# Value products in halves, the causal triangle inside the row maximum, and a moved turn of the maxima

## What is computed

```
att = einsum('bqhd,bkhd->bhqk', q, k) / sqrt(hd)      # L1_ffn, twice (f1, f2): 32 heads of 4, all keys
scores = einsum('bqhd,bkhd->bhqk', q, k) / sqrt(hd)   # L1_attn, L2_attn (a1, a2): 16 heads of 8
scores = scores + triu(-inf, k=1)                     # causal, in a1 and a2 alone
out = softmax(scores) @ v
```

## Time and profile before

| | us |
|---|---|
| runs | 3000.34, 3005.62, 3008.44 (median 3005.62) |
| profiled execution | 2999.32 |
| its span | 2997.6 |
| PE, PEld, DVE, ACT, POOL busy | 90%, 35%, 76%, 61%, 18% of the span |
| L1357 row maxima | 1566.9 us busy, 1536 instructions |
| L1232 exponentials | 1382.6 us busy, 2816 instructions |
| L972 value products | 712.9 us busy, 5632 instructions (an f32 product is two) |

### The profile page before, as it was taken

The page is one execution under the profiler, slowest core; times in us unless marked ns, Lnnn a source line. Parts: engine busy times, 40 slices in busy tenths (PEclk is TensorE's granted clock), DMA queues, the critical chain, the costliest instruction groups (busy, mean ns, idle before and its releaser), DMA issues. The chain is left out here.

```text
span 2997.6 us, 44120 instructions
## 1 busy us (share of the span) xinstructions
PE 2711.8 (90%) x16188; PEld 1052.7 (35%) x16188; DVE 2293.0 (76%) x3000; ACT 1830.7 (61%) x3731; POOL 530.3 (18%) x847
## 2 busy tenths in 40 slices
PE   5989898899999999889978999999998889979778
PEld 2437443122222222633332222222226433336336
DVE  5456545999999997667758999999984767765993
ACT  2213323588888888546655888888885656655203
POOL 0000001110111000122312110101001323222771
PEclk9999999799999999989987999999999889989989
DMA  3210121300000000221114000000000221100000
GB/s 116 85 62 2 53 89 56 120 20 20 20 20 20 18 14 25 79 64 47 39 31 138 20 20 16 16 20 20 20 18 21 78 63 39 39 29 29 0 0 16
DMA packets 71968, 120.38 MB, mean 40 GB/s; under 512 B 16905, under 2 KB 44041, under 8 KB 68586
## 3 DMA queue, kind: packets, MB, share of 16 engines
q1 hardware_dynamic: 71754, 117.57, 12.1%
HBM read 94.19 MB, written 23.33 MB: 39 GB/s over the span
## 5 line engine op out<-in xcount | busy, mean ns | idle before, releaser
L1357 DVE TENSOR_REDUCE arena<-ps 128x1 f32<-128x1024 f32 (+7 forms) x1536 | 1566.9, 1063 | 216.9 <-PE ps L952 136.9
L1232 ACT ACTIVATE arena<-ps 128x512 f32<-128x512 f32 (+3 forms) x2816 | 1382.6, 573 | 373.9 <-PE ps L1036 372.9
L946 PE MATMUL ps<-arena 61*128 61x512 bf16 (+4 forms) x2816 | 943.2, 383 | 42.7 <-DVE arena L1357 14.8
L1036 PE MATMUL ps<-arena 64*128 64x512 bf16 (+4 forms) x2816 | 746.8, 372 | 63.6 <-ACT arena L1232 40.4
L972 PE MATMUL ps<-arena 128*32 128x512 f32 (+3 forms) x5632 | 712.9, 578 | 0.4 <-POOL arena L1316 0.3
L1036 PEld LDWEIGHTS ps<-arena 64*128 64x128 bf16 (+1 forms) x2816 | 206.9, 95 | 788.3 <-ACT arena L1232 549.0
L946 PEld LDWEIGHTS ps<-arena 61*128 61x128 bf16 (+1 forms) x2816 | 261.2, 96 | 346.5 <-DVE arena L1357 284.0
L347 PE MATMUL ps<-xnT,moe_up 128*128 128x512 f32 x448 | 216.5, 609 | 0.0
L1285 POOL TENSOR_TENSOR arena<-arena,ones 16x128 bf16<-16x128 f32 x96 | 42.7, 445 | 953.9 <-ACT arena L1217 901.5
L463 ACT ACTIVATE arena<-ps 128x512 f32<-128x512 f32 x112 | 66.5, 597 | 208.0 <-PE ps L347 208.0
L533 DVE TENSOR_TENSOR arena<-arena,ps 128x512 f32<-128x512 f32 x112 | 76.5, 686 | 148.6 <-ACT arena L463 120.7
(11 more groups left out here) (241 smaller groups left out, 2504.5 us busy)
## 6 DMA issues: line engine op xcount, KB each, us to landing
arena<-m_w SPq DMA_DIRECT2D x40, 256.0 KB, 3.0
arena<-f_q SPq DMA_DIRECT2D x60, 144.0 KB
arena<-f_k SPq DMA_DIRECT2D x180, 48.0 KB
arena<-in_w SPq DMA_DIRECT2D x4, 2048.0 KB
arena<-a_q SPq DMA_DIRECT2D x14, 576.0 KB
arena<-a_k SPq DMA_DIRECT2D x42, 192.0 KB
a_q<-arena SPq DMA_DIRECT2D x44, 96.0 KB, 2.0
a_k<-arena SPq DMA_DIRECT2D x44, 96.0 KB, 2.0
```

What stands on the lines that cost most here:

```text
L946: last = nc.tensor.matmul(at[:, k0 // CHUNK, 0:n], score_rows(Qop[par], j, slice(q0, q0 + P)), score_rows(Kop[par], j, slice(k0, k0 + n)), ...
L1036: nc.tensor.matmul(ps[:, ring_bank(item), off:CHUNK], shifted_rows(Kop[par], j, slice(kb * P, (kb + 1) * P)), shifted_rows(Qop[par], j, sl ...
L1232: nc.scalar.activation(pr[:, (at % 2) * 4 + j, off:CHUNK], ps[:, ring_bank(item), off:CHUNK], ACT.Exp).then_inc(s.ex, 1)
L1357: nc.vector.tensor_reduce(mq[:, half, j * 4 + qb:j * 4 + qb + 1], src, AXX, ALU.max).then_inc(s.sread, 1)
```

## The change

Full layers: `ST_ORDER` becomes 0, 1, 2, 3. The AV of a step is split in two products of 256 queries each; the first is issued behind the second ST and its piece, the second at the end. An AV of key block 0 stays whole, at the end, since it starts the accumulation. All waits of an AV move to its first half; only the second half counts up `s.av`.

Causal layers: L952 is gone. The row maximum becomes one VectorE instruction that reads the scores (PSUM) and a bf16 tile `causal_add` (SBUF: zeros and the triangle), writes the sum back over the scores and gives its maximum. `causal_add` is made once per causal layer by a memset of 448 words and a copy of 128 columns.

Both: the turn is issued behind the piece or task that follows its score tile, not ahead of it.

```diff
--- before.py
+++ after.py
@@ -665,6 +665,7 @@
             mT = c(P)
             mr = c(P)
             ms = c(2 * 3 * P, BF16).rearrange("p (n a t) -> p n a t", n=2, a=3)
+            causal_add = None if full else c(SEQ, BF16)
 
             rot = c((4 if rope else 0) * CHUNK).rearrange("p (m n t) -> p m n t", m=2, n=2) if rope else None
             rem_at = c.at
@@ -872,7 +873,7 @@
                 for u in range(UNITS):
                     unit(u, u // 3, u % 3, u + 2 < UNITS, u + 1 < UNITS)
 
-            ST_ORDER = [0, 2, 1, 3] if SIDES == 2 else [0, 1, 2, 3]
+            ST_ORDER = [0, 1, 2, 3]
             S_ORDER = [2, 0, 3, 1] if SIDES == 2 else [0, 1, 2, 3]
 
             def s_tasks(half):
@@ -946,11 +947,7 @@
                         last = nc.tensor.matmul(at[:, k0 // CHUNK, 0:n],
                                                 score_rows(Qop[par], j, slice(q0, q0 + P)),
                                                 score_rows(Kop[par], j, slice(k0, k0 + n)), start=True,
-                                                stop=full or k0 + n < width)
-                    if not full:
-                        off = (width - P) % CHUNK
-                        last = nc.tensor.matmul(at[:, (width - 1) // CHUNK, off:off + P], identb[:, :],
-                                                maskb[:, 0, :], start=False, stop=True)
+                                                stop=True)
                     if piece != 0:
                         last.then_inc(s.s, 1)
 
@@ -960,21 +957,27 @@
                     nc.tensor.transpose(ps[0:16, bank, 0:P], mq[:, hn % 2, :], ident[:, :])\
                         .then_inc(s.mtp, 1)
 
-                def attend(u, vpar, at):
+                def attend(u, vpar, at, half=None):
                     qc, kb, off = steps[at]
-                    pe.wait_ge(s.ex, u * 4 * NS + 4 * at + 4 + 3)
+                    if half == 0 and kb == 0:
+                        return
+                    cols = slice(off, CHUNK) if half is None or kb == 0 else \
+                        slice(half * (CHUNK // 2), (half + 1) * (CHUNK // 2))
+                    if half != 1 or kb == 0:
+                        pe.wait_ge(s.ex, u * 4 * NS + 4 * at + 4 + 3)
                     if at in diagonal:
                         pe.wait_ge(s.tri, u * len(diagonal) + diagonal.index(at) + 1)
                     if kb == 0:
                         pe.wait_ge(s.vx, u + 1)
                         pe.wait_ge(s.ocp, 2 * u + qc + 1)
                     for j in range(GROUP):
-                        last = nc.tensor.matmul(ps[32 * j:32 * j + 32, O_BANK, off:CHUNK],
+                        last = nc.tensor.matmul(ps[32 * j:32 * j + 32, O_BANK, cols],
                                                 vx[vpar][:, kb, j, :],
-                                                pr[:, (at % 2) * 4 + j, off:CHUNK],
+                                                pr[:, (at % 2) * 4 + j, cols],
                                                 start=kb == 0, stop=at in ends,
                                                 tile_position=(0, 32 * j), skip_group_check=True)
-                    last.then_inc(s.av, 1)
+                    if half != 0:
+                        last.then_inc(s.av, 1)
 
                 def out_project(ch, n):
                     if n == 0:
@@ -1030,6 +1033,12 @@
                             n_task, piece = task
                             scores(n_task, piece=piece)
 
+                        def values_behind(half):
+                            if at:
+                                attend(u, par, at - 1, half)
+                            elif u:
+                                attend(u - 1, (par + 2) % 3, NS - 1, half)
+
                         for i, j in enumerate(ST_ORDER):
                             item = ("st", u * 4 * NS + 4 * at + i)
                             ring_free(pe, item)
@@ -1039,17 +1048,16 @@
                                 shifted_rows(Qop[par], j, slice(qc * CHUNK + off, (qc + 1) * CHUNK)),
                                 start=True, stop=True).then_inc(s.st, 1)
                             turn = ("turn", 2 * u + 1 + qc)
+                            if (SIDES == 2 or i % 2) and todo:
+                                run(todo.pop(0))
                             if (kb, i) == TURN_AT[qc] and turn in ring_at:
                                 ring_free(pe, turn)
                                 turn_max(turn[1], ring_bank(turn))
-                            if (SIDES == 2 or i % 2) and todo:
-                                run(todo.pop(0))
+                            if full and i == 1:
+                                values_behind(0)
                         while todo:
                             run(todo.pop(0))
-                        if at:
-                            attend(u, par, at - 1)
-                        elif u:
-                            attend(u - 1, (par + 2) % 3, NS - 1)
+                        values_behind(1 if full else None)
                         if u == UNITS - 1 and at >= NS - 2 * TPC:
                             out_project((at - NS + 2 * TPC) // TPC, (at - NS + 2 * TPC) % TPC)
                     if not ahead1:
@@ -1354,8 +1362,12 @@
                         b = score_bank(half, k)
                         width = SEQ if full else half * CHUNK + (qb + 1) * P
                         src = ps[:, b:b + 2, :].rearrange("p b t -> p (b t)")[:, 0:width]
-                        nc.vector.tensor_reduce(mq[:, half, j * 4 + qb:j * 4 + qb + 1], src, AXX,
-                                                ALU.max).then_inc(s.sread, 1)
+                        top = mq[:, half, j * 4 + qb:j * 4 + qb + 1]
+                        if full:
+                            nc.vector.tensor_reduce(top, src, AXX, ALU.max).then_inc(s.sread, 1)
+                        else:
+                            nc.vector.tensor_tensor_reduce(src, src, causal_add[:, SEQ - width:], 1.0, -3.0e38,
+                                                           ALU.add, ALU.max, top).then_inc(s.sread, 1)
 
                 def rotate(ch, side):
                     tt = slice((ch % 2) * CHUNK, (ch % 2 + 1) * CHUNK)
@@ -1390,6 +1402,9 @@
 
                 norm_chunk(dve, s, t, x_rows, 0)
                 norm_chunk(dve, s, t, x_rows, 1)
+                if not full:
+                    nc.vector.memset(causal_add[:, 0:SEQ - P].bitcast(F32), 0.0)
+                    t.settle(dve, nc.vector.tensor_copy(causal_add[:, SEQ - P:], maskb[:, 0, :]))
                 if rope:
                     dve.wait_ge(s.tab, 16)
                 cutting(0)
```

## The result

The changed kernel takes 2902.3 us (median of four runs, 2901.0 to 2904.1) against 3003.6 us before (four runs): a ratio of 0.966, 95% interval 0.964 to 0.968. The forecast was 2904. The profiled execution has a span of 2901.7 us.

The account below looks back on a forecast made before the run. It took the row-maximum loop (4.81 us per two steps), not an engine, to bound full layers, and mostly PE's queue causal ones. 2999.3 profiled - 92 full - 9 causal = 2898, or 2904 for the median; range 2882 to 2940.

Parts of the forecast that it names:

- The step: Full layers: a plain step of paired products and two half AVs ends at 2.21 us, where it took 2.40.
- The half: Full layers: six plain steps of 2.21, one with the turn 2.42, one with the copy 2.73: 18.41 us instead of 19.89.
- the maximum loop: Full layers before: row maxima, the products waiting for their slot and the AV form a loop, 4.81 us per two steps.
- the ring chain: Full layers before: AV start, ST0, its exponential, ST3 needing that bank, next AV: 2.39 us; not named by the prediction.
- the copy step: Full-layer step where the copy of the sums holds back exponentials and the AV stays undivided: 2.73 us, no gain.
- The cover: Full layers: first half AV wants the previous step's last exponential at 0.53, signalled by 0.47; lateness would come back in full.
- Rival 1: Full layers: first half AV waits for the last exponential, or products cost 0.05 more; -50 or less, 2945 to 2985; chance 0.16.
- The turn: Matmul turning the maxima, moved just ahead of the half AV in full layers: only its own 0.21 us remains, step 2.42.
- Masks: Causal layers: dropping 32 mask matmuls per unit saves 1.1 us per unit, 8 us per layer.
- Rival 2: Causal layers: the sum-and-maximum takes two passes per element, 2286 ns for 1024; 3092 us in all; chance 0.07.
- Rival 3: Full layers: pairs don't run side by side in the new order, a step of 3.1 us; chance 0.03 together with rival 4.
- rival 4: Full layers: halves are only added work, +0.23 on 512 steps, +118, 3115 us; chance 0.03 together with Rival 3.

Follow-up runs that it names:

- Half the maximum: Kernel before, with full layers' row maxima over the first 512 columns only and the exponential's input scaled by 0.001: 3003.3 us, ratio 1.000.
- the last run: Changed kernel with the two tasks of a causal step behind score tiles 0 and 2 instead of 1 and 3: 2889.1 us, ratio 0.961.
- the halves alone: Changed kernel's full layers with half AVs but old order 0, 2, 1, 3, turn ahead and causal layers as before: 3087.4 us, ratio 1.027.

## Why the prediction was right, and where not

- **The total.** 101 us were forecast and 101.3 measured. So close a hit is partly luck: the full layers gave 88 instead of 92, the causal ones 14.6 instead of 9, and the two errors cancel.
- **The step.** Pairs at 0, 0.23, 1.11, 1.33, half AVs at 0.53 and 1.64, end 2.21: each within 0.02. A half AV is 0.57, as the earlier trace rows had it.
- **The half.** 18.41 was forecast, 18.48 measured. The turn step is 2.46, not 2.42; the two steps that share the copy take 4.96, not 4.94. 0.07 more in each of 60 halves is 4 us, which is why the full layers gave 88, not 92, the term of the sum that was too large.
- **What bounded the kernel.** Half of it was missed. The prediction named the maximum loop (4.81) and not the ring chain (2.39), though its rows held both: it used 0.42 + 0.65 + 0.31 + 1.00 for the copy step and for the last unit's steps without tasks ("from 2.39"), and not for a plain step. Half the maximum changed nothing. The full layers' term came out right because it was built from the new step, in which the half AV falls into both chains; had the change been a faster maximum, the same reading would have promised some 80 us and got none. The 0.31 ahead of an AV was sized right, but its reason (it "needs all rows") is not the whole one: in the causal layers, where the tile ahead fills all rows too, the AV is 0.31 behind as well (1421.36 to 1421.66).
- **The cover.** It said that the last exponential's signal is there at 0.47 at the latest, for a half AV at 0.53. In the trace the last exponential of the step before begins at 905.47 and ends 0.60 later, at 906.07, 0.13 ahead of the half AV at 906.20, which starts on time. Rival 1 did not occur; how the kernel would behave with less cover, no run tested.
- **The turn.** Its new place was costed inside the step only. Put back, it costs 15.6 us, about a sixth of the gain.
- **The causal layers.** Masks: 1.1 per unit, and 1.10 it was, although the terms that the prediction lists (1.9 - 0.5 - 0.2) leave 1.2. The new maximum in the loop: +0.8 per layer forecast, at most 1.0 measured. The term that was wrong is the 2.6 us per layer ahead of the loop, 1.9 for the 32 maxima and 0.7 for `causal_add`. Making `causal_add` takes 0.48 us of DVE (1203.53 to 1204.00 in the trace of after), and neither shows in the time. From the start of the last exponential of the full layer to that of the first of the causal one, the seven traces with the old causal code take 102.8 and 150.5 us in the mean (first and second causal layer), the seven with the new code (in one of them the maximum is the plain one) 102.3 and 150.8. Together that is -0.2 us, where +5 was forecast; single traces differ by up to 3. So the 9 us forecast became 14.6 in the traces, and about 15 by the run of this part alone, whose interval does not reach below 10.
- **Rival 2** fell by one row: 1255 ns for 1024 columns, not 2286. **Rival 3** fell by the pairs, **rival 4** by the result; though the halves in the old order cost 82 us. The Trainium skill (Perfetto Trace Analysis, Matmuls) prefers larger matmuls; here it holds for the piece (2 x 0.57 against 1.00) and for the halves in the wrong order, not for the change, since PE's extra 0.23 a step is less than the two waits that it lifts. The other rule of the Trainium skill (VectorE: DVE Perf Modes, "Two Vector instructions with no wait between them"), an accumulator output is a second instruction, agrees with the trace: the 0.14 us row is it. Where maxima stand back to back they are 1.18 apart, against 1.14 of the plain ones, and of that 0.03 is the read.

## What to carry to other kernels

When a loop's length explains the step, look for a second chain of the same length before you believe that it is the bound: follow each waiting instruction on the engine, not only the first. Here shortening one gave nothing, shortening the other 23 us and shortening both 105. And when both are short, look once more at what waits: the step then stood at the ring chain again, not at PE's own work. On a PE that runs two halves of its rows at once, an instruction over all rows is a barrier: put all of them together, between complete pairs, and never between two pieces that hold one buffer.

## What the runs showed of the hardware

- Products come in three layouts here: on half the rows, over all rows, and over all rows in four column groups (the AV). Within a layout, products of 512 columns follow each other at 0.22 to 0.23; a change of layout costs 0.09 more. An AV starts 0.31 behind a product on half the rows (905.89 to 906.20 in after) and also 0.31 behind a tile over all rows in a causal layer (1421.36 to 1421.66 in the last run), so it is not only the rows. Nor is it the type f32: in the causal layers of the kernel before, the turn, f32 over all rows, starts 0.23 behind a tile over all rows, and the next product 0.11 behind the turn (1406.32, 1406.55, 1406.66); in the full layers, between products on half the rows, these are 0.31 and 0.21 (946.84, 947.15, 947.36). An unpaired product costs its whole 0.22.
- The sum-and-maximum over 1024 columns in PSUM, written back in place, takes 1255 ns (plain maximum 1214 to 1220); 896 columns take 1115, 512 take 725, 128 take 316. The accumulator read of 141 ns starts together with the next maximum and makes it 0.03 us longer (1.26 against 1.23 at 1024 columns, 0.33 against 0.30 at 128).
- In the kernel before, the ST of head 1 is issued behind T0b and starts ahead of it: the second ST of 904.64 against 904.86. A product on a free side does not wait for one issued earlier that waits for its own side; with a half AV between them (908.50 and 909.38 in the halves alone) it does.
